# A DLRM kernel's embedding gathers: the column that SyncE and ScalarE fetched row by row goes back to GpSimd

## The chip, the cores and the metric

One core of one Trainium2 chip. The metric is the device time of one execution in microseconds (us); the kernel before was timed in three runs.

## The reference

A recommendation model (DLRM) on a batch of 2048. For each sample, 26 integer indices pick 26 rows of 64 floats, each from its own table of 12,500 rows; a small two-layer network turns 13 dense numbers into a 27th vector of 64. All pairs of the 27 vectors give 351 dot products, and vectors and dot products go through three layers with ReLU and a last linear one. Everything is float32.

```
h = relu(dense @ dw1 + db1);  dense_emb = relu(h @ dw2 + db2)
sparse_emb = emb_tables[f_ids, sparse_idx]                 # (2048, 26, 64)
emb = concatenate([dense_emb[:, None, :], sparse_emb], 1)  # (2048, 27, 64)
inter = einsum('bfd,bgd->bfg', emb, emb);  pairs = inter[:, iu0, iu1]
z = concatenate([emb.reshape(2048, -1), pairs], 1)         # 1728 + 351
z = relu(z @ ow1 + ob1); z = relu(z @ ow2 + ob2); z = relu(z @ ow3 + ob3)
return z @ ow4 + ob4
```

## The kernel before

The batch is cut into 16 tiles of 128 samples (one sample in a partition). A tile's 26 embedding columns lie in `emb`, a ring of four tiles, as 13 pairs of two columns (128 floats). The pairs are worked on in four groups (`GROUPS`): pairs 0 to 3, 4 to 7, 8 to 11, and pair 12 alone, which holds columns 24 and 25.

**Gathers.** GpSimd (POOL) issues one indirect DMA per column and tile (L304); each reads 128 rows of 256 bytes, one per partition, at the row numbers that VectorE (DVE) worked out at the start. Each group of each ring place has a semaphore `gathered`, which PE waits on. The order on POOL is tile after tile, column after column. It holds waits on the tile before, so that POOL runs at most about a tile ahead: before columns 0, 16 and 24 for transposes of tile t-1, before column 4 for all transposes of tile t-1 (L297), before column 12 for the first half of tile t-1's dot products (L299), before column 16 for the second half (L292), before column 20 for the transposed pairs (L301).

**The exception.** In ten tiles (`OWN`: 2, 5, 7, 9, 11, 13, 15, 6, 10, 14) POOL leaves out column 25 (L302). Pair 12 of these tiles lies in a buffer of its own, `own`, with a place for each of the ten, so that nothing has to come free before it can be filled. Its second half is fetched by 128 plain DMAs of one row each, whose address comes from a register (`fetch`, L241 to L248: a group of register loads from SBUF, then one `dma_start` per row at L246). SyncE (SP) fetches those of seven tiles in order (896 rows, in groups of 32), with the loads of w2, w3 and w4 between the first 128 rows and the rest. ScalarE (ACT) fetches those of tiles 6, 10 and 14 (384 rows): 16 rows before and 16 rows after the evacuation of group 2 of each of the tiles 0 to 11 (`fetch_some`, L623, called at L654 and L657). The byte addresses are worked out by four DVE instructions on one partition, 1280 wide, in the start (L336 to L343), behind a small load of the indices (L260). Each of the ten has a semaphore `fetched`, on which PE waits before it transposes pair 12 (L709, L722).

```
SP_OWN = [2, 5, 7, 9, 11, 13, 15]
HELD = 32
ACT_OWN = [6, 10, 14]
ACT_ROWS = 16
```

**The rest of a tile.** PE transposes a group into PSUM (L712); ACT (groups 0 and 2, L508 and L516) and DVE (groups 1 and 3, L350 and L359) copy it out twice, once as `feat` for layer 1 and once as `slots` for the dot products. PE adds layer 1 in `features1` (L762, L771) as the copies come. Dot products are 64 small matmuls in two halves (L750), which both engines copy out (L528, L383); DVE turns them (L390), ACT picks the 351 pairs (L534, L540), PE transposes these (L733), DVE copies them out (L364), and PE adds them to layer 1 (L779). ACT applies the ReLU (L545), PE transposes the result (L786), and layers 2 to 4 run on four tiles at a time (L803, L808, L812), spread over later tiles. PE's order is written out by hand from L899 on: in tile t the transposes of group 0, the second half of the dot products of t-1, features 0 to 4, the pairs of t-1, the transposes of group 1, the turned hidden layer of t-1, features 5 to 8, the transposes of groups 2 and 3, features 9 to 13, the first half of the dot products of t. The last tile has an order of its own (L919 on), in which the remaining chain is cut finer.

Of the kernel before, what the change touches and what calls it, by code (L numbers as in the profile page):

```python
# [6 lines left out]

F32 = mybir.dt.float32
I32 = mybir.dt.int32
U8 = mybir.dt.uint8  # L10
U32 = mybir.dt.uint32
ALU = mybir.AluOpType
ACT = mybir.ActivationFunctionType
# [1 line left out]
P = 128  # L15
# [1 line left out]
GROUPS = [(0, 4), (4, 8), (8, 12), (12, 13)]  # L17
BATCHES = [(0, 4), (4, 8), (8, 12), (12, 14), (14, 15), (15, 16)]
LAST = BATCHES[-1][0]
SP_OWN = [2, 5, 7, 9, 11, 13, 15]  # L20
HELD = 32
ACT_OWN = [6, 10, 14]
ACT_ROWS = 16
OWN = SP_OWN + ACT_OWN
LAST_GROUPS = [(0, 4), (4, 8), (8, 10), (10, 12), (12, 13)]


def bass_dlrm_kernel(
# [1 line left out]
    dense_t: bass.AP,  # L30
    idx: bass.AP,
    first: bass.AP,
    own_idx: bass.AP,
    table: bass.AP,
    dw1: bass.AP,
    dw2: bass.AP,
# [33 lines left out]
    with ExitStack() as ctx:  # L70
# [16 lines left out]
        idx_f = sb("idx_f", [P, TILES, NF])  # L87
        rows = sb("rows", [P, TILES, NF], U32)
        emb = sb("emb", [P, RING, NP, 2 * D])
        own = sb("own", [P, len(OWN), 2 * D])  # L90
        own_raw = sb("own_raw", [1, len(OWN) * P], I32)
        own_f = sb("own_f", [1, len(OWN) * P])
        own_at = sb("own_at", [1, len(OWN) * P], U32)

        feat = [sb(f"feat{i}", [P, NP, P]) for i in range(2)]
        slots = [sb(f"slots{i}", [P, HALF, SETS, QUAD]) for i in range(2)]
# [79 lines left out]
        last_l4 = sem("last_l4")  # L176
        last_y = sem("last_y")

        own_in = sem("own_in")
        own_step = sem("own_step")  # L180
        own_rows = sem("own_rows")
        fetched = [sem(f"fetched{i}") for i in range(len(OWN))]

        w1_dram = ow1[D:D + NP * P, :].rearrange("(k p) n -> p k n", p=P)

        block = ctx.enter_context(nc.Block())
# [43 lines left out]
            return (tr_ps[0:PR, 0, 0:P], tr_ps[0:PR, 1, 0:P], l1_ps[0][0:PR, 0:P])[c]  # L230

        def pair_of(t, k):
            return own[:, OWN.index(t), :] if t in OWN and k == NP - 1 else emb[:, t % RING, k, :]

        def landed(t, n):
            a, b = GROUPS[n]
            return 16 * sum(2 * (b - a) - (n == NG - 1 and s in OWN) for s in range(t % RING, t + 1, RING))

        table_bytes = table.rearrange("r d -> (r d)").bitcast(U8)

        def fetch(eng, engine_type, a, b):  # L241
            _, at = nc.values_load_multi_w_load_instructions(  # L242
                own_at[0:1, a:b], engines=(engine_type,), min_val=0, max_val=(table.shape[0] - 1) * 4 * D,
                skip_runtime_bounds_check_because="DVE has clamped the rows")
            for r in range(a, b):
                eng.dma_start(own[r % P:r % P + 1, r // P, D:2 * D].bitcast(U8),  # L246
                              table_bytes[bass.ds(at[r - a], 4 * D)].rearrange("(o d) -> o d", o=1)
                              ).then_inc(fetched[r // P], 16)  # L248

        def upper_cols(b):  # L250
            return (BATCHES[b][1] - BATCHES[b][0]) * P
# [1 line left out]
        @block.sync  # L253
        def _(sp):
            sp.dma_start(first_sb[:], first).then_inc(first_in, 16)
            sp.dma_start(ident_sb[:], ident).then_inc(ident_in, 16)
            sp.dma_start(w1d_sb[:], ow1[0:D, :]).then_inc(w1d_in, 16)
            for n, (a, b) in enumerate(GROUPS):
                sp.dma_start(w1_sb[:, a:b, :], w1_dram[:, a:b, :]).then_inc(w1_in[n], 16)
            sp.dma_start(own_raw[:], own_idx).then_inc(own_in, 16)  # L260
            sp.dma_start(w1p_sb[:], ow1_pairs.rearrange("(c r) n -> r c n", r=PR)).then_inc(w1p_in, 16)

            sp.wait_ge(own_rows, 1)
            for first_row in range(0, P, HELD):
                fetch(sp, mybir.EngineType.SP, first_row, first_row + HELD)
            sp.dma_start(w2_sb[:], ow2.rearrange("(k p) n -> p k n", p=P)).then_inc(w234_in, 16)
            sp.dma_start(w3_sb[:], ow3.rearrange("(k p) n -> p k n", p=P)).then_inc(w234_in, 16)
            sp.dma_start(w4_sb[:], ow4).then_inc(w234_in, 16)
            for first_row in range(P, len(SP_OWN) * P, HELD):
                fetch(sp, mybir.EngineType.SP, first_row, first_row + HELD)  # L270

            for b, (a, e) in enumerate(BATCHES):
                if a == LAST:
                    sp.wait_ge(last_y, 1)
                else:
                    sp.wait_ge(upper_out, 4 * b + 4)
                sp.dma_start(out[a * P:e * P, :].rearrange("b o -> o b"), y[:, a * P:e * P]).then_inc(out_stored, 16)
            sp.wait_ge(out_stored, 16 * len(BATCHES))

        @block.gpsimd  # L280
        def _(pool):
            for t in range(TILES):
                pool.wait_ge(rows_in, min(t, 1) + 1)
                for n, (a, b) in enumerate(GROUPS):
                    if t >= 1:
                        if n == 0:
                            pool.wait_ge(transposed, t * NG - 2)
                            if t >= 2:
                                pool.wait_ge(h1_turned, t - 1)
                        elif n == 2:  # L290
                            pool.wait_ge(transposed, t * NG + 1)
                            pool.wait_ge(gram_done, 2 * t)  # L292
                        elif n == 3:
                            pool.wait_ge(transposed, t * NG + 2)
                    for c in range(2 * a, 2 * b):
                        if t >= 1 and c == 4:
                            pool.wait_ge(transposed, t * NG)  # L297
                        elif t >= 1 and c == 12:
                            pool.wait_ge(gram_done, 2 * t - 1)  # L299
                        elif t >= 1 and c == 20:  # L300
                            pool.wait_ge(pairs_turned, t)  # L301
                        if t in OWN and c == NF - 1:  # L302
                            continue
                        pool.indirect_dma_start(  # L304
                            out=pair_of(t, c // 2)[:, c % 2 * D:(c % 2 + 1) * D], out_offset=None, in_=table,
                            in_offset=bass.IndirectOffsetOnAxis(ap=rows[:, t, c:c + 1], axis=0),
                        ).then_inc(last_gathered[(c // 2 - a) // 2] if t == LAST and n == 2 else gathered[t % RING][n], 16)

        @block.vector
        def _(dve):  # L310
# [19 lines left out]
            for i in range(2):  # L330
                nc.vector.memset(slots[i][:, :, :, SLOTS:QUAD], 0.0).then_inc(consts_in, 1)
                nc.vector.memset(pairs_b[i][:, NPAIR:NPAIR + 1], 1.0).then_inc(consts_in, 1)
                nc.vector.memset(pairs_b[i][:, NPAIR + 1:PC * PR], 0.0).then_inc(consts_in, 1)
            dve.wait_ge(own_in, 16)
            w, v_rows = own_f[:], table.shape[0] // NF
            nc.vector.tensor_scalar(w, own_raw[:], 0.0, float(V), ALU.is_lt, ALU.mult).then_inc(own_step, 1)  # L336
            dve.wait_ge(own_step, 1)
            nc.vector.scalar_tensor_tensor(out=w, in0=own_raw[:], scalar=float(-V), in1=w,
                                           op0=ALU.max, op1=ALU.add).then_inc(own_step, 1)
            dve.wait_ge(own_step, 2)  # L340
            nc.vector.tensor_scalar(w, w, float(V - 1), float((NF - 1) * v_rows), ALU.min, ALU.add).then_inc(own_step, 1)
            dve.wait_ge(own_step, 3)
            nc.vector.tensor_scalar(own_at[:], w, float(4 * D), None, ALU.mult).then_inc(own_rows, 1)  # L343
            dve.wait_ge(dense_w_in, 4 * 16)

            def evac_features(t, n):
# [138 lines left out]
        def _(act):  # L485
# [134 lines left out]
                nc.scalar.activation(h2[:, 0, 0:P], last_ps(0)[:, 0:P], ACT.Relu,  # L620
                                     bias=bias_sb[:, OB2:OB2 + 1]).then_inc(last_h2[0], 1)

            def fetch_some(i):  # L623
                a, b = (min(x * ACT_ROWS, len(ACT_OWN) * P) for x in (i, i + 1))
                if i == 0:
                    act.wait_ge(own_rows, 1)
                if a < b:
                    fetch(act, mybir.EngineType.Activation, len(SP_OWN) * P + a, len(SP_OWN) * P + b)

            def last_hidden3():  # L630
                act.wait_ge(last_l3, 1)
                nc.scalar.activation(h3[:, 0:P], last_ps(2)[:, 0:P], ACT.Relu,
# [7 lines left out]
            for t in range(LAST):  # L640
# [10 lines left out]
                dense_slots(t)  # L651
                for stage in mid_stages(t):
                    upper_act(*stage)
                fetch_some(2 * t)  # L654
                evac_features(t, 2)
                group_slots(t, 2)
                fetch_some(2 * t + 1)  # L657
            gram_copies(14, 0)
            hidden3(3)
            gram_copies(14, 1)  # L660
# [24 lines left out]
        def _(pe):  # L685
# [12 lines left out]
            def transposes(t, n):  # L698
# [7 lines left out]
                if n == 3 and mid_stages(t):  # L706
                    pe.wait_ge(upper_out, out_count(mid_stages(t)[0]))
                pe.wait_ge(gathered[t % RING][n], landed(t, n))
                if t in OWN and n == NG - 1:  # L709
                    pe.wait_ge(fetched[OWN.index(t)], 16 * P)  # L710
                for k in range(a, b):
                    last = nc.tensor.transpose(tr_ps[:, n % 2, (k - a) * P:(k - a + 1) * P], pair_of(t, k),  # L712
                                               ident_sb[:])
# [2 lines left out]
            def last_transposes(n):  # L716
                a, b = LAST_GROUPS[n]
                if n in (2, 3):
                    pe.wait_ge(last_gathered[n - 2], 32 * (b - a))
                else:  # L720
                    pe.wait_ge(gathered[LAST % RING][3], landed(LAST, NG - 1))
                    if LAST in OWN:  # L722
                        pe.wait_ge(fetched[OWN.index(LAST)], 16 * P)
                for k in range(a, b):
                    last = nc.tensor.transpose(tr_ps[:, n % 2, (k - a) * P:(k - a + 1) * P], pair_of(LAST, k),
                                               ident_sb[:])
                last.then_inc(transposed, 1)
# [291 lines left out]
```

## Time and profile before

| | |
|---|---|
| time, median of 3 runs (lowest to highest) | 532.94 us (532.85 to 534.67) |
| span of the profiled execution, first to last instruction | 651.2 us |
| mean granted TensorE clock in it | 0.845 |
| PE matmul / POOL / DVE / ACT busy in it | 489.1 / 385.6 / 154.8 / 149.5 us |
| row fetches: SP, ACT | 896, 384 |
| gathers of POOL | 406 |

The profile is of one execution, and the page gives its span and no other time for it; it took 118 us longer than the median of the timed runs. Busy time of PE is from records whose ends are modelled. Where a releaser is called "remote", "issue" or "another core or an unknown queue", the profile saw no instruction end that explains the moment at which the wait was over.

### The profile page before, as it was taken

How to read it: one execution, taken by the hardware profiler on the slowest of the kernel's cores; microseconds unless marked ns; L12 is line 12 of the kernel's file. 1: busy time of each engine (PE TensorE's matmuls, PEld its weight loads, DVE VectorE, ACT ScalarE, POOL GpSimd, SP SyncE). 2: the span in 40 equal slices, each digit the busy share in tenths (PEclk: the TensorE clock that was granted, in tenths of full speed). 3: DMA queues.
4: the chain of work that ended last, by engine and by line, in shares of the span. 5: the costliest groups of instructions: out<-in, count | busy, mean ns of one | idle time of the engine just before them, and what ended most of it. 6: DMA issues, size and time to landing. Idle time of an engine off the chain costs nothing.

```text
span 651.2 us, 8430 instructions
## 1 busy us (share of the span) xinstructions
PE 489.1 (75%) x2262; PEld 259.7 (40%) x2262; DVE 154.8 (24%) x297; ACT 149.5 (23%) x337; POOL 385.6 (59%) x410
## 2 busy tenths in 40 slices
PE   6838857577695969867767887859767689796698
PEld 1314434243352535333333443424333244434577
DVE  1311303222122221402222131321212223041223
ACT  2212113121221303113130221312122131211323
POOL 6755656557566566656656666565656655663530
PEclk9967868779777988878897789789787799887799
DMA  8200010201011010110101011000100100100000
GB/s 264 67 21 24 23 24 22 60 22 26 19 24 23 23 23 24 24 23 22 24 22 25 21 25 23 20 23 22 25 21 24 23 22 21 26 23 11 22 17 3
DMA packets 19429, 19.56 MB, mean 30 GB/s; under 512 B 9760, under 2 KB 10787, under 8 KB 19369
## 3 DMA queue, kind: packets, MB, share of 16 engines
q0 software_dynamic: 12992, 13.33, 8.7%
q1 hardware_dynamic: 5202, 5.26, 2.6%
q10 hardware_dynamic: 1188, 0.44, 0.3%
q8 instruction: 18, 0.29, 0.2%
q14 instruction: 29, 0.24, 0.1%
HBM read 18.99 MB, written 0.01 MB: 29 GB/s over the span
## 4 chain that ended last, share of the span: by engine, by line
PE 29%; issue 25%; ACTq 13%; SPq 10%; another core or an unknown queue 10%; ACT 8%; DVE 4%; DMA 1%
ACTq L246 12%; SPq L246 9%; PE l_ps L771 8%; PE gram_ps L750 6%; PE l_ps L779 5%; PE tr_ps L803 3%; ACT gram_c L528 2%; ACT slots L516 1%; SPq L242 1%; ACT feat L508 1%; PE l_ps L866 1%; PE gram_ps L803 1%; PE gram_ps L866 1%; ACT pairs_b L540 1%
## 5 line engine op out<-in xcount | busy, mean ns | idle before, releaser
L304 POOL DMA_INDIRECT emb<-table_dram,rows x396 | 375.9, 949 | 235.9 <-issue 108.3
L771 PE MATMUL l_ps<-w_sb,feat 128*128 128x512 f32 x390 | 218.6, 714 | 71.6 <-ACT feat L508 69.7
L771 PEld LDWEIGHTS l_ps<-w_sb,feat 128*128 128x128 f32 x390 | 85.4, 229 | 188.2 <-issue 113.1
L383 DVE COPY gram_c<-gram_ps 32x432 f32<-32x432 f32 x60 | 36.6, 609 | 238.1 <-remote 131.2
L750 PE MATMUL gram_ps<-slots 64*128 64x108 f32 x960 | 72.0, 309 | 27.3 <-DVE gram_c L383 20.4
L750 PEld LDWEIGHTS gram_ps<-slots 64*128 64x128 f32 x960 | 66.3, 217 | 42.2 <-DVE gram_c L383 22.2
L528 ACT COPY gram_c<-gram_ps 32x432 f32<-32x432 f32 x60 | 30.5, 509 | 183.9 <-remote 106.0
L779 PE MATMUL l_ps<-w1p_sb,pairs 118*128 118x512 f32 x90 | 59.5, 813 | 10.0 <-issue 5.9
L350 DVE COPY feat<-tr_ps 128x512 f32<-128x512 f32 (+1 forms) x32 | 15.7, 492 | 166.2 <-remote 76.6
L508 ACT COPY feat<-tr_ps 128x512 f32<-128x512 f32 (+1 forms) x32 | 18.4, 575 | 151.7 <-issue 73.2
L516 ACT COPY slots<-tr_ps 64x256 f32<-64x256 f32 (+1 forms) x128 | 50.4, 394 | 1.1
L359 DVE COPY slots<-tr_ps 64x256 f32<-64x256 f32 (+1 forms) x124 | 42.9, 346 | 1.3
L712 PEld LDWEIGHTS tr_ps<-ident_sb,emb 128*128 128x128 f32 x194 | 25.3, 149 | 33.6 <-issue 33.1
L779 PEld LDWEIGHTS l_ps<-w1p_sb,pairs 118*128 118x128 f32 x90 | 21.5, 255 | 36.8 <-issue 31.9
L712 PE MATMUL tr_ps<-ident_sb,emb 128*128 128x128 f32 x194 | 32.1, 287 | 4.5 <-DMA emb<-table_dram,rows 3.1
L545 ACT ACTIVATE h<-l_ps 128x512 f32<-128x512 f32 x15 | 9.0, 597 | 88.4 <-issue 48.1
L390 DVE STREAM_TRANSPOSE gram_b<-gram_c 128x864 f32<-128x864 f32 x15 | 27.9, 1860 | 0.5
L803 PE MATMUL tr_ps<-h1t,w_sb 128*128 128x512 f32 x48 | 24.2, 634 | 4.0 <-issue 4.0
L733 PE MATMUL tr_ps<-ident_sb,pairs_b 128*118 128x128 f32 x45 | 8.6, 307 | 19.0 <-issue 11.3
L762 PE MATMUL l_ps<-w1d_sb,dense_e 64*128 64x512 f32 x30 | 20.5, 772 | 0.0
L364 DVE COPY pairs<-tr_ps 118x384 f32<-118x384 f32 x15 | 8.4, 558 | 37.3 <-PE tr_ps L733 28.5
L733 PEld LDWEIGHTS tr_ps<-ident_sb,pairs_b 128*118 128x118 f32 x45 | 5.4, 149 | 29.1 <-issue 29.1
(114 smaller groups left out, 225.4 us busy)
## 6 DMA issues: line engine op xcount, KB each, us to landing
own<-table_dram SPq DMA_DIRECT2D x896, 0.2 KB
emb<-table_dram,rows POOLq DMA_INDIRECT x396
own<-table_dram ACTq DMA_DIRECT2D x384, 0.2 KB
w_sb<-ow_dram SPq DMA_DIRECT2D x3, 1024.0 KB
w1p_sb<-ow_pairs_dram SPq DMA_DIRECT2D x1, 708.0 KB
w_sb<-ow_dram SPq DMA_DIRECT2D x1, 512.0 KB
w_sb<-ow_dram SPq DMA_DIRECT2D x1, 256.0 KB
idx_raw<-idx_dram ACTq DMA_DIRECT2D x1, 208.0 KB
```

Of the source, the lines that this page charges most:

```text
L246: eng.dma_start(own[r % P:r % P + 1, r // P, D:2 * D].bitcast(U8), table_bytes[bass.ds(at[r - a], 4 * D)].rearrange("(o d) -> o d", o=1)). ...
L304: pool.indirect_dma_start(out=pair_of(t, c // 2)[:, c % 2 * D:(c % 2 + 1) * D], out_offset=None, in_=table, in_offset=bass.IndirectOffsetO ...
L359: last = nc.vector.tensor_copy(slots[t % 2][h * D:(h + 1) * D, :, :, base:base + b - a], src[:, h])
L383: last = nc.vector.tensor_copy(dst, src)
L390: nc.vector.transpose(gram_b[t % 2][:, 0:SLOTS, :], gram_c[:].rearrange("p i g -> p g i")).then_inc(gram_turned, 1)
L516: last = nc.scalar.copy(slots[t % 2][h * D:(h + 1) * D, :, :, base:base + b - a], src[:, h])
L528: last = nc.scalar.copy(dst, src)
L712: last = nc.tensor.transpose(tr_ps[:, n % 2, (k - a) * P:(k - a + 1) * P], pair_of(t, k), ident_sb[:])
L750: mm = nc.tensor.matmul(gram_ps[:, bank, r * GCOLS:(r + 1) * GCOLS], x.rearrange("p c f -> p (c f)"), x[:, :, 0:SLOTS], start=True, stop=True)
L771: nc.tensor.matmul(l1_ps[t % 2][:], feat[t % 2][:, n - 1, :], w1_sb[:, n - 1, :], start=False, stop=False)
L779: mm = nc.tensor.matmul(l1_ps[t % 2][:], pairs[t % 2][:, c, :], w1p_sb[:, c, :], start=False, stop=c == PC - 1)
L803: mm = nc.tensor.matmul(upper_ps(b, s)[:, 0:n], w2_sb[:, k, s * P:(s + 1) * P], h1t[b % 2][:, k, 0:n], start=(k == 0), stop=(k == M1 - 1))
```

## The change

The ten exceptions go. POOL gathers all 26 columns of all 16 tiles, every pair lies in the ring `emb`, and the buffer, the index load, the four DVE instructions, all 1280 row fetches with their register loads, the ten semaphores and PE's waits on them are gone. Nothing else in any engine's order changes. The diff, without the lines that only drop declarations and the host's array:

```
@@ top
-SP_OWN = [2, 5, 7, 9, 11, 13, 15]
-HELD = 32
-ACT_OWN = [6, 10, 14]
-ACT_ROWS = 16
-OWN = SP_OWN + ACT_OWN
@@ helpers
         def pair_of(t, k):
-            return own[:, OWN.index(t), :] if t in OWN and k == NP - 1 else emb[:, t % RING, k, :]
+            return emb[:, t % RING, k, :]
         def landed(t, n):
             a, b = GROUPS[n]
-            return 16 * sum(2 * (b - a) - (n == NG - 1 and s in OWN) for s in range(t % RING, t + 1, RING))
+            return 32 * (b - a) * (t // RING + 1)
-        def fetch(eng, engine_type, a, b):
...
@@ SP
-            sp.dma_start(own_raw[:], own_idx).then_inc(own_in, 16)
             sp.dma_start(w1p_sb[:], ow1_pairs.rearrange("(c r) n -> r c n", r=PR)).then_inc(w1p_in, 16)
-            sp.wait_ge(own_rows, 1)
-            for first_row in range(0, P, HELD):
-                fetch(sp, mybir.EngineType.SP, first_row, first_row + HELD)
             sp.dma_start(w2_sb[:], ow2.rearrange("(k p) n -> p k n", p=P)).then_inc(w234_in, 16)
             sp.dma_start(w3_sb[:], ow3.rearrange("(k p) n -> p k n", p=P)).then_inc(w234_in, 16)
             sp.dma_start(w4_sb[:], ow4).then_inc(w234_in, 16)
-            for first_row in range(P, len(SP_OWN) * P, HELD):
-                fetch(sp, mybir.EngineType.SP, first_row, first_row + HELD)
@@ POOL
-                        if t in OWN and c == NF - 1:
-                            continue
@@ DVE
-            dve.wait_ge(own_in, 16)
-            w, v_rows = own_f[:], table.shape[0] // NF
-            nc.vector.tensor_scalar(w, own_raw[:], 0.0, float(V), ALU.is_lt, ALU.mult).then_inc(own_step, 1)
...
-            nc.vector.tensor_scalar(own_at[:], w, float(4 * D), None, ALU.mult).then_inc(own_rows, 1)
@@ ACT, per tile
-                fetch_some(2 * t)
                 evac_features(t, 2)
                 group_slots(t, 2)
-                fetch_some(2 * t + 1)
@@ PE, transposes and last_transposes
-                if t in OWN and n == NG - 1:
-                    pe.wait_ge(fetched[OWN.index(t)], 16 * P)
```

## Rows read from the trace of the kernel before

**Rows 1.** The page: span, busy times, then 40 slices of the span.
```profile
span 651.2 us, 8430 instructions
PE 489.1 (75%) x2262; PEld 259.7 (40%) x2262; DVE 154.8 (24%) x297; ACT 149.5 (23%) x337; POOL 385.6 (59%) x410
...
PEclk9967868779777988878897789789787799887799
DMA  8200010201011010110101011000100100100000
```
**Rows 2.** Instructions grouped by line, POOL: xcount | busy us, mean ns | idle before.
```profile
L304 POOL DMA_INDIRECT emb<-table_dram,rows x396 | 375.9, 949 | 235.9 <-issue 108.3 <-remote 64.8 <-PE gram_ps L750 30.7
L304 POOL DMA_INDIRECT own<-table_dram,rows x10 | 9.5, 945 | 6.3 <-issue 6.3
```
**Rows 3.** Timeline of POOL, tile 12 into 13: start us, us, instruction, [idle before].
```profile
505.21 0.95 POOL L304 DMA_INDIRECT emb<-table_dram,rows  x1 [0.30 <-issue]
506.46 0.95 POOL L304 DMA_INDIRECT emb<-table_dram,rows  x1 [0.30 <-issue]
...
513.35 0.95 POOL L304 DMA_INDIRECT emb<-table_dram,rows  x1 [2.19 <-remote]
...
525.32 0.94 POOL L304 DMA_INDIRECT emb<-table_dram,rows  x1 [2.27 <-remote]
```
**Rows 4.** Timeline of POOL, its first gather, those beside DVE's address work, its last.
```profile
3.75 1.08 POOL L304 DMA_INDIRECT emb<-table_dram,rows  x1 [3.29 <-DVE rows L327]
...
16.39 1.48 POOL L304 DMA_INDIRECT emb<-table_dram,rows  x1 [0.30 <-issue]
18.17 1.36 POOL L304 DMA_INDIRECT emb<-table_dram,rows  x1 [0.30 <-issue]
19.83 1.24 POOL L304 DMA_INDIRECT emb<-table_dram,rows  x1 [0.30 <-issue]
21.38 0.94 POOL L304 DMA_INDIRECT emb<-table_dram,rows  x1 [0.30 <-issue]
...
627.04 0.95 POOL L304 DMA_INDIRECT own<-table_dram,rows  x1 [0.30 <-issue]
```
**Rows 5.** Timeline of SP and ACT: row fetches, and ACT's next copy.
```profile
22.44 101.72 SPq L246 DMA_DIRECT2D own<-table_dram  x128
...
236.08 8.63 ACTq L246 DMA_DIRECT2D own<-table_dram  x14
244.76 0.59 ACT L508 COPY feat<-tr_ps 128x512 f32<-128x512 f32 x1 [9.72 <-issue]
...
600.00 9.62 SPq L246 DMA_DIRECT2D own<-table_dram  x17
```
**Rows 6.** Waits of PE: who waited for whom, us in total, times, longest.
```profile
PE l_ps L771 <- ACT feat L508: 69.7, 13, 7.8
...
PE tr_ps L712 <- DMA own<-table_dram: 7.3, 1, 7.3
```
**Rows 7.** Timeline of PE in tiles 5 and 12, behind a wait for ACT's copy.
```profile
245.40 6.93 PE L771 MATMUL l_ps<-w_sb,feat 128*128 128x512 f32 x10 [6.04 <-ACT feat L508]
...
504.47 3.70 PE L771 MATMUL l_ps<-w_sb,feat 128*128 128x512 f32 x8
508.00 0.71 PE L712 MATMUL tr_ps<-ident_sb,emb 128*128 128x128 f32 x5
513.72 7.60 PE L771 MATMUL l_ps<-w_sb,feat 128*128 128x512 f32 x10 [5.00 <-ACT feat L508]
```
**Rows 8.** Timeline of DVE: the four address instructions.
```profile
16.23 0.81 DVE L336 TENSOR_SCALAR own_f<-own_raw 1x1280 f32<-1x1280 int32 x1 [4.78 <-issue]
17.07 1.48 DVE L338 SCALAR_TENSOR_TENSOR own_f<-own_raw,own_f 1x1280 f32<-1x1280 int32 x1
...
19.44 0.82 DVE L343 TENSOR_SCALAR own_at<-own_f 1x1280 uint32<-1x1280 f32 x1
```

More of the change, by code:

```diff
@@ L9 @@
 I32 = mybir.dt.int32
-U8 = mybir.dt.uint8
 U32 = mybir.dt.uint32
@@ L32, in bass_dlrm_kernel @@
     first: bass.AP,
-    own_idx: bass.AP,
     table: bass.AP,
@@ L89, in bass_dlrm_kernel @@
         emb = sb("emb", [P, RING, NP, 2 * D])
[L90 to L93, printed above, removed]
         feat = [sb(f"feat{i}", [P, NP, P]) for i in range(2)]
@@ L177, in bass_dlrm_kernel @@
         last_y = sem("last_y")
[L179 to L182, printed above, removed]
         w1_dram = ow1[D:D + NP * P, :].rearrange("(k p) n -> p k n", p=P)
@@ L232, in pair_of @@
         def pair_of(t, k):
-            return own[:, OWN.index(t), :] if t in OWN and k == NP - 1 else emb[:, t % RING, k, :]
+            return emb[:, t % RING, k, :]
         def landed(t, n):
             a, b = GROUPS[n]
-            return 16 * sum(2 * (b - a) - (n == NG - 1 and s in OWN) for s in range(t % RING, t + 1, RING))
-        table_bytes = table.rearrange("r d -> (r d)").bitcast(U8)
-        def fetch(eng, engine_type, a, b):
[L242 to L248, printed above, removed]
+            return 32 * (b - a) * (t // RING + 1)
         def upper_cols(b):
@@ L333, in _ @@
                 nc.vector.memset(pairs_b[i][:, NPAIR + 1:PC * PR], 0.0).then_inc(consts_in, 1)
-            dve.wait_ge(own_in, 16)
-            w, v_rows = own_f[:], table.shape[0] // NF
-            nc.vector.tensor_scalar(w, own_raw[:], 0.0, float(V), ALU.is_lt, ALU.mult).then_inc(own_step, 1)
[L337 to L342, printed above, removed]
-            nc.vector.tensor_scalar(own_at[:], w, float(4 * D), None, ALU.mult).then_inc(own_rows, 1)
             dve.wait_ge(dense_w_in, 4 * 16)
@@ L621, in last_hidden2 @@
                                      bias=bias_sb[:, OB2:OB2 + 1]).then_inc(last_h2[0], 1)
[L623 to L628, printed above, removed]
             def last_hidden3():
@@ L721, in last_transposes @@
                     pe.wait_ge(gathered[LAST % RING][3], landed(LAST, NG - 1))
-                    if LAST in OWN:
-                        pe.wait_ge(fetched[OWN.index(LAST)], 16 * P)
                 for k in range(a, b):
@@ L998 @@
         "first_dram": _np.concatenate([base, idx[:, 0], last_row], axis=1),
-        "own_idx_dram": _np.concatenate([idx[:, t, NF - 1] for t in OWN])[None],
         "table_dram": table.reshape(-1, D),
```

## The prediction

> **What bounds the kernel now.** I began with the page [rows 1]. PE looks like the bound (489 us busy of 651), POOL far from it (386), and the DMA engines are nearly idle after the start. But the profiled span is 118 us longer than the timed median of 532.94, so shares of this span are not shares of the run that is timed. The question is which part of the profiled span can be absent from a timed run.
>
> Next, POOL's instructions by line [rows 2] and its timeline [rows 3]. A gather is recorded as 0.95 us, and where nothing holds it up the next one starts 1.25 us after it (505.21 to 506.46): 0.30 us always lies between. All 406 gathers without any wait take 385.4 + 406 × 0.30 = 507.2 us. Their recorded idle time is 235.9 + 6.3 = 242.2 us; less the fixed 121.8 and the 3.3 before the first gather [rows 4], 117.1 us are real waits of POOL. They come at the waits written into its order: for all transposes of the tile before (513.35) and for the first half of the dot products (525.32), some 2 us each [rows 3].
>
> Now put POOL without waits end to end: first gather at 3.75, 507.2 us of gathers, and behind the last one (627.04 + 0.95 = 627.99) the 23.2 us to the end of the span, in which PE, ACT and DVE finish the last tile [rows 1, 4]. That is 534 us, the same as 651.2 − 117.1, and 1.2 us from the timed median. So I read the timed run as one in which POOL issues gathers without pause from start to end, and PE keeps up. The profiled run differs in that PE's results come late: in tile 12 five transposes are recorded from 508.00 to 508.71, but ACT's copy of them, and with it PE's next features, begins at 513 [rows 3, 7]. What delays them the trace doesn't say, and the sum says that timed runs have nearly none of it. It could be chance that two numbers meet; this is the rivals' opening.
>
> **The change part by part.** The sum is made on the profiled run with its POOL waits taken out (534 us), which lies 0.2% above the median; I then carry the difference to 532.94.
>
> *Ten more gathers on POOL.* 10 × 1.25 = 12.5 us [rows 3]. No row shows less than that pitch. POOL is on the path throughout by the reading above, so all of it counts. The addition in tile 15 also delays the last tile's end directly: the last gather is now column 25, and pair 12 waits for it. The lower bound of this term is 0, if POOL waits for PE as long in timed runs as here; the upper bound is 12.5 plus new waits, see the rivals. I take 12.5, because the sum leaves no room for waits.
>
> *Four DVE instructions less at the start.* They are recorded from 16.23 to 20.26 [rows 8], and just the three gathers started beside them take 1.48, 1.36 and 1.24 us in place of 0.95 [rows 4]: 1.2 us lost on POOL, which the change gives back. The Trainium skill, page "SBUF — State Buffer", section "SBUF: two separate sides", says that VectorE copies of fp32 within SBUF lock GpSimd out of the ports it needs for writing descriptors; here the trace agrees, and both make the time 1.2 us shorter. On DVE itself the work is hidden, since its next instruction waits for the transposes of tile 0.
>
> *1280 row fetches less, SP.* SP's stream begins at 22.44 and ends at 609.62 [rows 5]: 587 us. It cannot last so long in a run of 533, so timed runs issue rows faster. Nothing on SP waits for tiles, and only w2 to w4 and the results lie behind the rows; w2 to w4 now load at the start instead of at 124, which PE doesn't need before tile 4. I cost this at nothing for PE except the one wait for tile 2's rows (7.3 us [rows 6]). In the timed run that wait cannot be much more than a microsecond, or the sum would be above the median. Zero taken; 7.3 is the bound of a gain.
>
> *1280 row fetches less, ACT.* 16 rows hold ACT for about 9 us (236.08 on [rows 5]), twice in each of twelve tiles, and PE waits for the copy behind (6.04 us in tile 5). But tile 12, where ACT fetches nothing, has the same wait with 5.00 us [rows 7]. So the fetches cost PE about 1.0 us per tile, 12 us in twelve tiles, within the slack that PE has against POOL. It counts 0 while POOL is the bound. If that cover is gone it is 12 us of gain.
>
> *Ring and waits.* Pair 12 of ten tiles moves from its own buffer into the ring. POOL already waits for the transposes of tile t-1 before it writes there, so the ring adds no wait, and PE's `fetched` waits go without a successor except the gather itself. It lands at most one pitch later than column 24 did, which is the 1.25 already counted. The removed 1280 transfers leave DMA engines that were at a tenth of their time [rows 1]: nothing.
>
> Sum: 12.5 − 1.2 = +11.3 us; 532.9 + 11.3 = **544.2 us**. (On the basis of 534: 545.3.)
>
> About 0.5% (2.7 us) is what a measurement of this kernel can tell from no change, so "same" is 530.3 to 535.6.
>
> **The rivals.**
>
> *PE sets the pace in the timed run too, and POOL's added gathers go into its waits.* For it: in the profiled run POOL waits 117 us, over 7 per tile, against 0.8 us of added gathers per tile. Then the ten gathers cost nothing and the time is 532.9 less the 1.2, about 532. Against it: gathers of 1.25 us plus such waits don't fit into 533 us; it needs a pitch in timed runs well below the one recorded. The Trainium skill, page "DMA: Bandwidth & Descriptors", section "Issuing engines are not separate DMA queues", says that issuing from several engines saves only the sequencer's time for it, usually small beside the DMA itself; by that the exception was worth nothing and the time would stay near 532. Here the issue time is just what POOL is full of. Chance 7%.
>
> *Faster, by ACT and SP set free.* The mechanism: PE waits at L771 for ACT's copy of group 2 because ACT issues rows, and at tile 2 for SP's rows. Its price is the 12 us above and up to 7.3: 532.9 − 12 = 521, or 514 with both. It decides once POOL's floor lies below the present time: 26.9 us (3.7 before and 23.2 behind) + 416 × pitch < 532.9, that is a pitch under 1.216 us against the 1.25 recorded. For it: SP's rows show that queue work is faster in timed runs than recorded. Against: the mean gather of 949 ns over 396 of them [rows 2] and the 0.30 behind each leave no slow stretch that a timed run could do without. Chance 8%.
>
> *Slower by more, through the clock.* PE's work per tile stays and the tile gets longer, so it idles more, and features 9 to 13 run at the lower clock more often: in tile 12 ten records take 7.60 us after an idle time of 5 us, where eight took 3.70 before it [rows 7]; the mean grant is at two levels mixed. Ten records at the pace of the eight would be 4.6, so 3.0 us more per tile. If that turns POOL's free waits in the ten tiles into real ones, it is +30 beside the 11.3: 574 at worst, 555 for half of it. Against: in the timed run POOL's eight gathers between the two waits (10 us) cover that chain. Chance 4%.
>
> **How the numbers follow.** The forecast, POOL as the bound in both kernels, has 81%: 538 to 550 with its own uncertainties. Below 544.2: part of the 7.3 of tile 2 or of the slow start, where ACT's first rows delay tile 0. Above: some of the clock's cost in the tail, which no gather covers. The range 537.5 to 550 leaves out the rivals, 19% together. All of the forecast is slower, and so is the clock's case: 0.85 slower, 0.07 same, 0.08 faster.
>
> **What would show it.** Right: 416 gathers at 1.25 us pitch; the gathers at 16 to 20 us at 0.95; timed median minus 416 × 1.25 about 25 us, as 532.9 − 507.2 was. If recording the 1280 fetches was what made the profiled run late, its span falls from 651 to near the timed value, and POOL's waits vanish; if not, it stays at 640 to 655. Either fits the forecast. Wrong: a median under 536, which would mean that POOL had waits in timed runs and that the pitch there is shorter than recorded; or over 550, with POOL's waits before columns 12 and 16 longer and the clock lower.

## The result and the profile after

The kernel after takes 543.99 us (median of four runs, 543.03 to 545.27), the kernel before beside it 532.89: a ratio of 1.0213, 95% interval 1.0196 to 1.0231. It is slower by 11.1 us; the forecast was 11.3. Medians in this document are of all executions of a kernel; ratios leave out those that were more than 1.5% above the fastest of the same kernel, which occur only on one chip, C below.

The profile of the kernel after, its page: span, busy times, part of the slices, and the chain that ended last.

```profile
span 542.9 us, 5816 instructions
PE 450.7 (83%) x2262; PEld 239.9 (44%) x2262; DVE 150.9 (28%) x293; ACT 150.2 (28%) x337; POOL 394.0 (73%) x420
...
POOL 6777777777777777777777777777777777777740
PEclk9988979789897979979798898989979799999989
...
POOL 58%; issue 22%; PE 15%; DMA 3%; DVE 1%; ACT 1%; POOLq 0%
```

Two things are unlike before [rows 1]. The span agrees with the timed runs (the profiled run itself took 544.75 us, 1.85 more than its span). And POOL's row of digits is flat: seven tenths in every slice between the first and the last two, which is 0.95 us of gather in each 1.25. The chain names POOL, and "issue" is the 0.30 between its gathers. PE's busy share is larger, yet PE isn't the bound.

POOL's instructions by line, which answers to rows 2:

```profile
L268 POOL DMA_INDIRECT emb<-table_dram,rows x416 | 393.8, 947 | 129.5 <-issue 124.7 <-DVE rows L291 3.0 <-PE l_ps L727 1.5
```

POOL's waits: engine, line, what it waited for, us in total, times, longest:

```profile
POOL emb L268 <- issue: 124.7, 409, 0.3
POOL emb L268 <- PE l_ps L727: 1.5, 5, 0.3
```

The idle time of 129.5 us is the 3.0 at the start and 415 gaps of 0.305: POOL waits for nobody. No gap is longer than the fixed 0.3, so the 1.5 us put down to PE are five of these gaps and no real waits. The timeline of POOL, its start and its end (answers to rows 4):

```profile
3.45 1.08 POOL L268 DMA_INDIRECT emb<-table_dram,rows  x1 [3.00 <-DVE rows L291]
...
9.83 1.30 POOL L268 DMA_INDIRECT emb<-table_dram,rows  x1 [0.30 <-issue]
...
16.44 0.94 POOL L268 DMA_INDIRECT emb<-table_dram,rows  x1 [0.30 <-issue]
...
522.81 0.94 POOL L268 DMA_INDIRECT emb<-table_dram,rows  x1 [0.30 <-issue]
```

The longest of PE's waits (answers to rows 6), and behind it the same wait in the profile of before:

```profile
PE tr_ps L655 <- DMA emb<-table_dram,rows: 64.1, 35, 4.1
...
PE tr_ps L712 <- DMA emb<-table_dram,rows: 3.1, 2, 2.0
```

The timeline of PE in tile 5, features 9 to 13 behind the transpose of pair 12 (answers to rows 7):

```profile
200.29 0.45 PE L655 MATMUL tr_ps<-ident_sb,emb 128*128 128x128 f32 x1 [1.40 <-DMA emb<-table_dram,rows]
200.53 6.56 PE L712 MATMUL l_ps<-w_sb,feat 128*128 128x512 f32 x10
```

The last gather starts at 522.81 and 19.2 us remain behind its end. PE now waits 64 us for gathered rows (before, 3 us on the profiled run), which is the picture of an engine that is fed too slowly, and its wait for ACT's copy (69.7 us [rows 6]) is gone.

**The profile before was of another behaviour.** The page of the kernel before shows a span of 651.2 us beside timed runs of 533. The experiments found out what that was: of the chips that ran these kernels, one runs the kernel before at 646 us, and its profile there looks like rows 1 to 7; two others run it at 532 us. So the rows ahead of the prediction are most likely a true picture, but of a chip on which PE's results come late, while the timed runs were made where they don't. The record doesn't name the chip of that first profile, so this is a conclusion and not a measurement. The kernel before was never profiled on a chip where it takes 532 us: what it does there is concluded from kernels close to it. Experiments are grouped by chip below, called A (before: 532.24 us), B (532.17) and C (646.52).

### The profile page after: what moved, and what is told of

The parts are those of the page before. It is cut to its first block, busy times and chain, and to the rows that moved or that the text cites. A ratio compares the mean times of both kernels' runs of the same rounds, so it can differ in the third digit from the quotient of the medians.

```text
span 542.9 us, 5816 instructions
## 1 busy us (share of the span) xinstructions
PE 450.7 (83%) x2262; PEld 239.9 (44%) x2262; DVE 150.9 (28%) x293; ACT 150.2 (28%) x337; POOL 394.0 (73%) x420
## 4 chain that ended last, share of the span: by engine, by line
POOL 58%; issue 22%; PE 15%; DMA 3%; DVE 1%; ACT 1%; POOLq 0%
POOL emb L268 58%; PE l_ps L712 5%; DMA emb<-table_dram,rows 3%; PE l_ps L720 3%; PE gram_ps L691 2%; PE l_ps L703 1%; PE tr_ps L744 1%; PE tr_ps L655 1%; PE l_ps L727 1%; ACT h L499 1%; DVE pairs L318 1%; PE tr_ps L674 0%; PE l_ps L807 0%; PE tr_ps L769 0%; DMA first_sb<-first_dram 0%
## 5 line engine op out<-in xcount | busy, mean ns | idle before, releaser
L268 POOL DMA_INDIRECT emb<-table_dram,rows x416 | 393.8, 947 | 129.5 <-issue 124.7
L712 PE MATMUL l_ps<-w_sb,feat 128*128 128x512 f32 x390 | 207.1, 682 | 0.9 <-DVE feat L304 0.9
L655 PE MATMUL tr_ps<-ident_sb,emb 128*128 128x128 f32 x203 | 39.7, 315 | 65.5 <-DMA emb<-table_dram,rows 64.1
L691 PEld LDWEIGHTS gram_ps<-slots 64*128 64x128 f32 x960 | 58.2, 194 | 14.7 <-issue 14.1
L691 PE MATMUL gram_ps<-slots 64*128 64x108 f32 x960 | 63.4, 284 | 0.3 <-DVE gram_c L337 0.3
L462 ACT COPY feat<-tr_ps 128x512 f32<-128x512 f32 (+1 forms) x32 | 18.5, 578 | 125.8 <-PE tr_ps L655 124.9
L720 PE MATMUL l_ps<-w1p_sb,pairs 118*128 118x512 f32 x90 | 42.6, 609 | 9.8 <-DVE pairs L318 9.8
L720 PEld LDWEIGHTS l_ps<-w1p_sb,pairs 118*128 118x128 f32 x90 | 15.9, 189 | 27.8 <-issue 15.3
L703 PE MATMUL l_ps<-w1d_sb,dense_e 64*128 64x512 f32 x30 | 16.6, 634 | 0.0
L744 PEld LDWEIGHTS tr_ps<-h1t,w_sb 128*128 128x128 f32 x48 | 8.7, 189 | 9.6 <-issue 9.1
L727 PE MATMUL l_ps<-ident_sb,h 128*128 128x128 f32 x60 | 9.8, 287 | 3.7 <-ACT h L499 3.7
```

Of the source, the lines that this page charges most:

```text
L268: pool.indirect_dma_start(out=pair_of(t, c // 2)[:, c % 2 * D:(c % 2 + 1) * D], out_offset=None, in_=table, in_offset=bass.IndirectOffsetO ...
L691: mm = nc.tensor.matmul(gram_ps[:, bank, r * GCOLS:(r + 1) * GCOLS], x.rearrange("p c f -> p (c f)"), x[:, :, 0:SLOTS], start=True, stop=True)
L703: nc.tensor.matmul(l1_ps[t % 2][:], dense_e[:, t * P:(t + 1) * P], w1d_sb[:], start=True, stop=False)
L712: nc.tensor.matmul(l1_ps[t % 2][:], feat[t % 2][:, n - 1, :], w1_sb[:, n - 1, :], start=False, stop=False)
L720: mm = nc.tensor.matmul(l1_ps[t % 2][:], pairs[t % 2][:, c, :], w1p_sb[:, c, :], start=False, stop=c == PC - 1)
L744: mm = nc.tensor.matmul(upper_ps(b, s)[:, 0:n], w2_sb[:, k, s * P:(s + 1) * P], h1t[b % 2][:, k, 0:n], start=(k == 0), stop=(k == M1 - 1))
```

## Experiments on chip A: does the number of gathers set the time?

**Ten gathers left out of the kernel after** (no fetches either):

```
+LEFT_TILES = [4, 5, 6, 7, 9, 10, 11, 13, 14, 15]
+LEFT_COLS = [25]
+                        if t in LEFT_TILES and c in LEFT_COLS:
+                            continue
```

> The kernel after, with column 25 of ten tiles (4, 5, 6, 7, 9, 10, 11, 13, 14, 15) not gathered at all: 406 gathers as before, no row fetches, no address work on DVE. Those parts of emb keep the rows of four tiles earlier, so the output is not the reference's. Theory (POOL's count of gathers sets the time, row fetches cost the timed run nothing): 544.0 - 10 x 1.25 = 531.5 us, which is the kernel before less the 1.2 us that DVE took from POOL at the start. Rival (the fetches held up ACT and PE in the kernel before, so part of the loss in the change is hidden by that gain): also about 531.5, as the count is what acts now, but then before should stand well above it, by 5 us or more.

Measured: 530.57 us, 0.9971 of before (0.9960 to 0.9983). Without its fetches and the address work, a kernel with before's 406 gathers is 1.7 us faster than before. In its profile no gap between gathers is longer than the fixed 0.3. So whatever the fetches, the address work and waits for rows cost before there is some 1.7 us together, and the rival, which wanted 5 us or more, is out on this chip.

**DVE's address work kept, nothing fetched** (the index load and the four instructions put back into the kernel after).

> The kernel after, with the index load and the four DVE address instructions of before kept, and nothing fetched. Theory: the three gathers beside them take 0.5, 0.4 and 0.3 us longer, so 544.0 + 1.2 = 545.2 us. Rival (the DVE work is hidden): 544.0 and gathers of 0.95 at 16 to 20 us.

Measured: 543.65 us, 1.0216 of before (1.0202 to 1.0229). The kernel after was not beside it on this chip; its ratios elsewhere are 1.0213 and 1.0205, so by the times the work costs about 0.2 or 0.6 us. Each of these ratios has an interval of 0.7 us or more to either side, so the times alone exclude neither nothing nor the 1.2 of the prediction. The timeline of POOL shows the three long gathers all the same:

```profile
9.90 0.94 POOL L297 DMA_INDIRECT emb<-table_dram,rows  x1 [0.30 <-issue]
...
16.13 1.27 POOL L297 DMA_INDIRECT emb<-table_dram,rows  x1 [0.30 <-issue]
17.71 1.36 POOL L297 DMA_INDIRECT emb<-table_dram,rows  x1 [0.30 <-issue]
19.37 1.24 POOL L297 DMA_INDIRECT emb<-table_dram,rows  x1 [0.30 <-issue]
```

They lose 1.0 us. But here the gather at 9.90 took 0.94, where the kernel after has one of 1.30 at 9.83, beside the instructions with which DVE works out the row numbers for the other 15 tiles. How a gather and a DVE instruction meet is a matter of a few tenths of a microsecond at the start, and it differs from run to run. The last gather starts at 522.95 here and at 522.81 there.

**All 26 columns on POOL and all 1280 fetches kept**, with nobody waiting for them but SP at the very end:

```
-                        if t in OWN and c == NF - 1:
-                            continue
-                if t in OWN and n == NG - 1:
-                    pe.wait_ge(fetched[OWN.index(t)], 16 * P)
+            for i in range(len(OWN)):
+                sp.wait_ge(fetched[i], 16 * P)
```

> The kernel before, except that POOL also gathers column 25 of the ten tiles into emb and nobody waits for the rows that SP and ACT fetch into the old buffer (SP waits for them at the very end). 416 gathers, 1280 row fetches. Theory (fetches are hidden in the timed run, and it is only their recording that makes the profiled run late): timed 545.2 us as with the DVE work alone, with a profiled span of 640 us or more. Rival (1280 fetches cost the timed run on ACT, PE or the DMA engines, up to 12 us, and POOL's waits in the profile are real): timed 550 to 557.

Measured: 544.45 us, 1.0232 of before (1.0218 to 1.0246), 0.8 us above the kernel with the DVE work alone. On the time the theory holds. On the profile it fell: the span was 542.2 us, not 640. Recording the fetches does not by itself stretch a profile. The instructions of its line 246 (duration in ns, lowest, median and highest, and the first and last start):

```profile
L246 SPq DMA_DIRECT2D own<-table_dram x896: 224/228/461, 22.4 to 378.2; - x180
```

Its timeline of SP:

```profile
22.40 48.45 SPq L246 DMA_DIRECT2D own<-table_dram  x128
```

Its timeline of ACT in tile 1, from the rows to the copy of group 2:

```profile
63.62 5.23 ACTq L246 DMA_DIRECT2D own<-table_dram  x16
70.73 0.59 ACT L508 COPY feat<-tr_ps 128x512 f32<-128x512 f32 x1 [7.30 <-PE tr_ps L710]
```

SP's first 128 rows take 48 us here against 101.72 [rows 5], and all 896 are done by 378, 160 us before the end. ACT's 16 rows take 5.2 us in tile 1 and end 1.9 us before the copy can start, which then waits for PE's transposes: they are hidden. In the whole profile PE never waits for this copy.

**Ten gathers more** (column 24 of ten tiles once more, into a spare buffer), 426 in all:

```
+                        if t in AGAIN and c == NF - 2:
+                            pool.indirect_dma_start(
+                                out=spare[:, AGAIN.index(t), :], out_offset=None, in_=table,
+                                in_offset=bass.IndirectOffsetOnAxis(ap=rows[:, t, c:c + 1], axis=0),
+                            ).then_inc(again, 16)
```

> The kernel after with ten more gathers, column 24 of the ten tiles once more into a spare buffer, 426 in all. Theory: 544.0 + 10 x 1.25 = 556.5 us, the same step as the change made. Rival (POOL has slack in the timed run, and the change cost what it did by something else, say the later last gather): under 550.

Measured: 556.70 us, 1.0459 of before (1.0441 to 1.0476). Between this kernel and the one with ten left out lie 20 gathers and 26.1 us, 1.31 us each. In their traces the last gathers start 25.4 us apart; the rest is in the tail. The last gather with ten more, and behind it the last with ten left out:

```profile
534.94 0.94 POOL L273 DMA_INDIRECT emb<-table_dram,rows  x1 [0.30 <-issue]
...
509.57 0.94 POOL L273 DMA_INDIRECT emb<-table_dram,rows  x1 [0.30 <-issue]
```

The rival that POOL had slack is out on this chip.

## Experiments on chip B: what the fetches cost, and where the pattern ends

The kernel after, and beside it the one with all fetches kept.

> The kernel after, unchanged, the partner of the next one on this chip. Chips differ: on one the kernel before takes 532 us and its POOL never waits, on another 646 us, with PE, SP and ACT issuing instructions 0.7 us apart in stretches. Theory: where before is near 532, this is 543.3 (POOL's count). Where before is near 646, it is about 634 again, 2% faster, because PE and not POOL sets the pace there.

> All 26 columns gathered by POOL, and the 1280 row fetches kept with nobody waiting for the rows until the end. Where before is near 532: 1 us above the kernel after (0.4 of DVE's work on POOL, the rest of the fetches). Where before is near 646, theory A (the instructions of the fetches themselves slow the issue of the other engines, or hold ACT up): near 646, as slow as before. Theory B (PE's waits for the fetched rows are what costs there): near 634, as fast as after.

Measured: after 542.64 us, 1.0205 of before (1.0191 to 1.0219); with the fetches 544.57, 1.0242 (1.0220 to 1.0263). DVE's work and 1280 fetches together cost 1.9 us, more than the 1 expected; their ranges touch (542.2 to 544.1 and 543.5 to 546.5). All of it is on POOL: its last gather starts at 523.89 with the fetches and at 521.78 without, though it waits for nobody in either; 0.9 of these 2.1 us are the three gathers beside DVE's work, the rest is spread over the start and many small steps. With chip A's step of 1.7 us this agrees: to keep the exception costs between 1 and 2 us, and it buys ten gathers.

**Four more exceptions**, to look for a version better than both:

```
-SP_OWN = [2, 5, 7, 9, 11, 13, 15]
+SP_OWN = [2, 4, 5, 7, 9, 10, 12, 13, 15]
-ACT_OWN = [6, 10, 14]
-ACT_ROWS = 16
+ACT_OWN = [3, 6, 8, 11, 14]
+ACT_ROWS = 24
```

> The kernel before with four more exceptions: SP fetches column 25 of nine tiles, ACT of five, 24 rows at a time; POOL issues 402 gathers. Where before is near 532: theory (POOL's count, rows of SP take 0.3 to 0.4 us each and are in time) 532.2 - 5.0 = 527.2 us, faster than both kernels; rival (tile 2's or 3's rows are late, or ACT is held up) 530 or more. Where before is near 646: slower than before, by theory A of the kernel beside it.

Measured: 546.50 us, 1.0277 of before (1.0263 to 1.0291), slower than both. The rival was right, and by more than it said. Waits of ACT, PE and POOL:

```profile
ACT feat L508 <- issue: 103.8, 12, 8.9
...
PE l_ps L771 <- ACT feat L508: 45.4, 13, 5.1
...
POOL emb L304 <- PE gram_ps L750: 18.5, 15, 2.4
```

ACT's timeline in tile 2:

```profile
98.63 7.96 ACTq L246 DMA_DIRECT2D own<-table_dram  x24
106.62 0.58 ACT L508 COPY feat<-tr_ps 128x512 f32<-128x512 f32 x1 [8.66 <-issue]
```

ACT now issues rows for 8 us, where the transposes need it after about 7 (the 7.30 us of idle time before its copy in the profile of chip A). The copy of group 2 starts as soon as the rows are out: twelve times the idle time before it ends with "issue", not with PE. PE waits 45 us for ACT, where with 16 rows at a time and all 416 gathers it waited for none. The first half of the dot products comes late, and POOL waits for that before column 12. Of the 18.5 us listed, 15 × 0.30 are the fixed gaps; added up over its whole timeline, POOL's gaps exceed the fixed ones by 16 us, against the 5 it saved. DVE's four instructions are 1792 wide here and stretch the three gathers beside them to 1.43, 2.86 and 1.51 us, 3.0 us in place of 1.2. The parts give −5.0 + 16 + 1.8 = +12.8, measured +14.3; 1.5 us are not explained. The 16 rows of the kernel before were about what ACT can hide.

**84 gathers left out** (seven columns of tiles 4 to 15):

> The kernel after with seven columns of each of the tiles 4 to 15 not gathered (332 gathers; emb keeps older rows there, the output is not the reference's). It shows where PE takes over. Where before is near 532: POOL alone would need 544 - 105 = 439 us; PE's records are 451 us busy in the kernel after, and with its waits for copies I expect 470 to 490. Where before is near 646: about 620 to 634, as POOL has long had slack there.

Measured: 479.44 us, 0.9014 of before (0.9002 to 0.9026). The POOL row by line:

```profile
L273 POOL DMA_INDIRECT emb<-table_dram,rows x332 | 313.4, 944 | 141.6 <-issue 95.5 <-PE gram_ps L696 32.3 <-PE tr_ps L660 9.9
```

The time is in the expected range. From 406 to 332 gathers a gather brings (530.57 − 479.44) / 74 = 0.69 us (two chips with the same time of before), and POOL's gaps exceed the fixed 0.30 by 38 us, nearly all of it in waits for PE. So on these chips each gather less counts in full at first (1.31 us around 416) and only in part on the way to 332; where between 406 and 332 PE takes over was not measured.

## Experiments on chip C: where PE's results come late

The kernel before was profiled again, with the kernel after and the two halves of the exception beside it.

> The kernel before, unchanged, profiled once more. Its first profiled execution took 651.2 us, in which SP and ACT issued rows at 0.7 us each and POOL waited 117 us for PE; the kernel with all 26 columns and the same 1280 fetches was profiled at 542.2 us, with rows at 0.3 to 0.4 us and no wait of POOL. Theory (that one execution was disturbed, and the timed runs never look like it): span 530 to 533, POOL at its 1.25 pitch throughout, waits under 5 us, rows of SP ended by about 380. Rival (fetches into a buffer that PE waits on do cost, under the profiler at least): span about 650 again.

> The kernel after, unchanged, on the same chip as the kernels beside it, where the kernel before stands at 532.2: the one with DVE's address work kept gave 543.65 and the one with all fetches kept 544.45 us. Theory: about 543.3, so that DVE's work is worth a third of a microsecond and the fetches 0.8. By the term of the prediction (1.2 us for DVE's work) it would be 542.5.

> The kernel before without ACT's share: SP fetches column 25 of seven tiles, POOL gathers it in tiles 6, 10 and 14, 409 gathers. Theory (1.25 us per gather, ACT's fetches hidden): 532.2 + 3.75 = 536.0 us, up to 0.4 less for the fewer fetches. Rival (ACT's fetches hold PE up in timed runs): under 534, as ACT is set free.

> The kernel before without SP's share: ACT fetches column 25 of three tiles, POOL gathers it in the other seven, 413 gathers. Theory: 532.2 + 8.75 = 541.0 us, up to 0.8 less for the fewer fetches and the shorter address work. Rival (the last gather, column 25 of the last tile, costs the tail more than a pitch, as nothing hides its landing): above 542.5.

Measured: before again 644.21 us, 1.0002 (0.9965 to 1.0038) of its twin's 646.52; **after 633.87, 0.9865 (0.9796 to 0.9935): here the change makes the kernel faster**; SP's seven alone 641.72, 0.997 (0.992 to 1.0019), no difference that can be told; ACT's three alone 647.68, which leaves open whether it differs (one execution took 632.9, the other five 643.5 to 652.4). The theories of all four expectations missed, as none had counted with such a chip. The first one's rival (a span of about 650 again) came near in number, with 642.9, but not for the reason it gave, as the kernel after, without any fetch, is slow here too. Of before again, POOL's instructions by line:

```profile
L304 POOL DMA_INDIRECT emb<-table_dram,rows x396 | 375.7, 949 | 227.9 <-issue 107.6 <-remote 62.3 <-PE gram_ps L750 32.2
```

And its timeline of SP:

```profile
22.18 100.11 SPq L246 DMA_DIRECT2D own<-table_dram  x128
```

They are rows 2 and 5 again, to a few per cent, and all 35 executions of the kernel before on this chip took 638 us or more: the behaviour belongs to the chip (or to its state in that hour), it is not the accident of one execution. And of the kernel after on this chip, PE in the dot products of one tile:

```profile
232.82 1.81 PE L691 MATMUL gram_ps<-slots 64*128 64x108 f32 x28
235.28 0.25 PE L691 MATMUL gram_ps<-slots 64*128 64x108 f32 x1 [0.64 <-issue]
235.99 0.35 PE L691 MATMUL gram_ps<-slots 64*128 64x108 f32 x1 [0.46 <-issue]
237.38 0.34 PE L691 MATMUL gram_ps<-slots 64*128 64x108 f32 x1 [1.04 <-issue]
238.79 0.54 PE L691 MATMUL gram_ps<-slots 64*128 64x108 f32 x1 [1.07 <-issue]
239.51 1.01 PE L744 MATMUL tr_ps<-h1t,w_sb 128*128 128x512 f32 x1 [0.18 <-issue]
```

The 32 records of such a half take 2.04 us in a piece in the profile shown first (tile 5, at 207.02). Here the last four come 0.7 or 1.4 us apart, and PE waits for nothing that the profile shows; rows of SP in the kernel before on this chip come in steps of 0.7 us too. Nothing was fetched by SP or ACT in this kernel, so the fetches don't cause it. POOL's gather is 946 ns here too, and ACT's copy of 577 ns is what it was (578). What is slow is the spacing of PE's and SP's instructions, and the granted clock is lower (0.843 against 0.912); I read the spacing as slow issue, which no run shows as such, and what makes it slow is not known. POOL's waits in this kernel:

```profile
POOL emb L268 <- issue: 116.0, 371, 1.0
POOL emb L268 <- remote: 58.4, 23, 4.4
POOL emb L268 <- PE tr_ps L674: 13.4, 9, 1.9
```

Its gaps exceed the fixed 0.30 by 85 us in all, so POOL has slack here. That fits ten more gathers being hidden and the exception costing without buying anything, though ten gathers alone were not added or left out on this chip. Why the exception costs 9 to 13 us there (the first by the ratio, the second by the medians) is not settled. The gain of leaving all of it out (1.35%) is clear; neither half alone showed one. Whether the number of instructions, ACT's time or PE's waits for the rows make it up was not tried on this chip: the kernel that tells them apart ran on A and B.

## Why the prediction was right, point by point

- *POOL without a pause is the timed run.* Right, and shown for the chips that run before at 532 us: no wait in the profile after, none in the one with 406 gathers and no fetches, and +10 or −10 gathers move the time by 12 to 14 us. For the kernel before itself it follows from that second kernel, which is only 1.7 us faster; no profile of it on such a chip exists. The sum of 534 that led to the reading was partly luck. "534 us, the same as 651.2 − 117.1" is one sum taken in two ways, so only its nearness to 532.94 said anything. The sum counted 23.2 us behind the last gather, from the slow profile; the kernel after has 19.2, and the timed run has 1.85 us beyond its span that the sum left out.
- *Ten gathers, 12.5 us.* Right in size. The step is 12.1 us from 530.57 on chip A to 542.64 on chip B (before at 532.2 on both).
- *DVE's instructions, −1.2 us.* Probably somewhat too large: 0.2 to 0.6 by the times on chip A, which are too coarse to settle it, and 0.9 to 1.0 in the three gathers of the profiles on chips B and A, against 1.2 in rows 4. That such instructions lengthen the gathers beside them is shown by the experiment that put them back. The section of the Trainium skill named in the prediction speaks of copies of fp32 within SBUF, and these four are no copies; the lock that the Trainium skill describes was not tested by itself. In some runs without them a gather beside another DVE instruction comes out longer instead (1.30 us at 9.83 in the kernel after). I counted one meeting of the two engines and not the others.
- *Fetches of SP and ACT, 0.* Nearly right: DVE's work and the fetches cost 1.7 and 1.9 us together where POOL sets the pace. That timed runs issue rows faster than rows 5 was right (0.38 us per row in place of 0.79 over the first 128). That the cover over ACT's part is thin, 1.9 us in tile 1, was not seen from the profile before: with 24 rows it was gone.
- *What made the profiled run late.* I left this open and named the recording of the fetches as one way. That was wrong: with all fetches recorded the span was 542.2, and on chip C the timed runs are late as well.
- *The rival in which PE sets the pace in timed runs too.* It had 7%. It is what happens on chip C, though there the time falls by 1.35% rather than staying. The argument against it (gathers and waits don't fit into 533 us) was sound for the runs that were timed; it didn't ask whether every chip is like them. The section "Issuing engines are not separate DMA queues" of the Trainium skill, page "DMA: Bandwidth & Descriptors", speaks of the issue time as the only thing won. The runs agree, with the number beside it: that time is 1.25 us a gather here, and where POOL is full it is all that counts. The Trainium skill also calls that time usually small beside the DMA itself; here it is not, as a gather takes 2.4 us from issue to landing (median in the profile after). Ten gathers moved off POOL were worth about 12 us on chips A and B, not nothing.
- *The rival in which ACT and SP set free make it faster.* It had 8%. Its condition, a pitch under 1.216 us, was met nowhere: the pitch is 1.25 in every trace. Chip C does get faster, by an amount near its 12 us, but on a chip with slack on POOL, and leaving out ACT's share alone brought no gain that can be told there. So the mechanism of this rival is not shown.
- *The clock.* The rival of 555 to 574 did not come: on chips A and B and in the first comparison the granted clock is 0.91 to 0.93 with 416 gathers and 0.92 to 0.94 with 406. By its own sum, half of its 30 us would have been 559 and not 555.

## What to carry to other kernels

When a profiled span and the timed median differ by a fifth, first find the engine whose instructions alone, laid end to end, give the timed number; price the change on that engine, and take a second profile before trusting a wait of the first. An engine that issues gathers back to back makes each one cost its full pitch, so moving even 1 of 26 pays, but only as long as the helper's own issue time is shorter than the gap it had (5.2 us of 7 paid, 8 did not). And what the same kernel gains on one chip can be lost on another: the change costs 2.1% in two comparisons, on chips where before takes 532 us, and gains 1.35% on another, so the comparison has to be made on the chip it is for.

## What the runs showed of the hardware that was not expected

- One core of one chip ran the same kernel 21% slower (646.5 against 532.2 us) over 23 runs. The instructions of DVE, ACT and POOL that carry the work took the same time in the kernel after (ACT's copy 577 and 578 ns, a gather 946 and 947); SP issued row fetches at 0.78 us instead of 0.38 (128 rows in 100.11 and 48.45 us), and in stretches PE instructions came one by one, 0.7 us or a multiple apart. What causes it is open.
- On that chip copies that wait for PE begin up to 9.8 us after the last matmul record they wait for starts (DVE's copy of the dot products' first half, tiles 2 to 13 of the kernel after; always 0.32 us in the profile shown first). The ends of PE's records are modelled, so I read such a lag, which the profile calls "remote", as the trace of matmuls that ran later than they stand; no run shows that directly.
- A gather is 0.95 us and the next starts 1.25 us after it, as the median of each of the fourteen traces, on all three chips, with and without row fetches on the other queues. Gathers longer than that (1.15 to 1.51 us, once 2.86) are found only beside DVE's instructions at the start, one to four times in eleven of the fourteen traces and in none of the other three; putting four such instructions back brought three of them. How much a gather is stretched differs between traces of the same kernel.
